# A decoder layer's long convolution: columns ordered feature first, gathering copies on ScalarE, ternary weights in 48 pieces

## What is computed

```
x = x + attention(layernorm(x))                       # 16 query heads, 4 value heads
x = x + conv(ctx, ctx, layernorm(x))                  # 32 heads of 8 rows, 64 x 512 in all
x = x + ffn(layernorm(x))                             # 512 -> 2048 -> 512

# conv, one head, l runs over 512 positions (the context is transposed into them):
kv[i, j, l] = k[i, l] * v[j, l]                       # here k = v, so (i, j) and (j, i) agree
y[i, j]     = causal_conv(kv[i, j], ssm_kernel[h]) + D[h] * kv[i, j]
out[j, l]   = sum_i y[i, j, l] * q[i, l]

# ffn: weights w -> clip(round(w / mean|w|), -1, 1) * mean|w|; activations to 8 bits
```

## Time and profile before

| what | value |
|---|---|
| median of 3 runs (lowest, highest) | 736.14 us (735.43, 736.41) |
| the profiled execution | 736.74 us, span of its instructions 734.9 us |
| busy over the span | PE 86%, DVE 76%, ACT 60%, POOL 36% |
| mean granted TensorE clock | 0.96 |

### The profile page before, as it was taken

How to read it: one execution, slowest core, us unless ns; L and a number is a source line. 1 busy time by engine, 2 the same in 40 slices (tenths; PEclk the granted TensorE clock), 3 DMA queues, 4 the chain that set the end, 5 groups by cost and what they waited for, 6 DMA issues and landing times.

```text
span 734.9 us, 10711 instructions
## 1 busy us (share of the span) xinstructions
PE 635.0 (86%) x3055; PEld 354.8 (48%) x3074; DVE 556.8 (76%) x981; ACT 440.3 (60%) x751; POOL 265.3 (36%) x248
## 2 busy tenths in 40 slices
PE   5899999999999988877778787974789999999995
PEld 3435454554545434655556565652344444444442
DVE  3465756767583644488787888999999999999983
ACT  2446675676667551666666666421676767767781
POOL 1001010000100030555554555642565655656672
PEclk9969999999999969999999999995999999999998
DMA  9535072543618150444535544220001011010001
GB/s 315 143 136 116 1 229 50 178 100 128 171 57 229 44 143 0 153 159 132 181 118 148 170 130 124 85 86 15 15 16 58 29 43 43 29 57 29 15 30 43
DMA packets 34245, 72.51 MB, mean 99 GB/s; under 512 B 4336, under 2 KB 16112, under 8 KB 32560
## 3 DMA queue, kind: packets, MB, share of 16 engines
q1 hardware_dynamic: 31056, 60.72, 28.0%
q10 hardware_dynamic: 3168, 11.54, 4.9%
HBM read 47.51 MB, written 4.28 MB: 70 GB/s over the span
## 4 chain that ended last, share of the span: by engine, by line
DVE 26%; issue 11%; ACT 9%; POOL 6%; PE 5%; ACTq 1%; DVEq 1%; POOLq 0%
POOL big L790 6%; DVE qo L758 4%; ACT wst L848 4%; DVE toep L1184 3%; DVE xq L1170 3%; DVE mb L1188 3%; PE ps L1061 2%; PE ps L1049 2%; DVE act8t L1220 2%; ACT wt L852 2%; ACT ys L829 2%; DVE x_all L1133 1%; DVE mx L1155 1%; DVE xn L1151 1%; DVE st L1138 1%
## 5 line engine op out<-in xcount | busy, mean ns | idle before, releaser
L705 PE MATMUL ps<-kv,toep 128*128 128x288 f32 x640 | 165.4, 416 | 35.5 <-DVE big L750 33.5
L705 PEld LDWEIGHTS ps<-kv,toep 128*128 128x128 f32 x640 | 121.4, 193 | 79.6 <-issue 47.7
L1061 PE MATMUL ps<-wt,xqt 128*128 128x512 bf16 x496 | 122.1, 389 | 11.1 <-DVE toep L1184 9.5
L758 DVE TENSOR_REDUCE qo<-big 128x2048 f32 (+1 forms) x32 | 124.2, 3881 | 0.0
L1313 POOL TENSOR_TENSOR big<-toep,wst 128x512 f32<-128x512 f32 x64 | 81.6, 1276 | 59.5 <-DVE toep L1184 59.4
L393 ACT ACTIVATE big<-ps,kscale 128x512 f32<-128x512 f32 x128 | 85.2, 696 | 13.6 <-PE ps L243 11.9
L243 PE MATMUL ps<-qx,kx 128*128 128x512 f32 x128 | 78.2, 639 | 11.2 <-ACT big L393 10.4
L790 POOL TENSOR_TENSOR big<-ys,qd 128x768 f32<-128x768 f32 x32 | 55.4, 1732 | 85.9 <-ACT ys L830 68.6
L1061 PEld LDWEIGHTS ps<-wt,xqt 128*128 128x128 bf16 x512 | 48.6, 100 | 67.0 <-DVE toep L1184 11.2
L747 DVE TENSOR_TENSOR big<-ps,qd 128x1024 f32<-128x1024 f32 x32 | 39.1, 1223 | 38.2 <-ACT ys L830 37.3
L1049 PE MATMUL ps<-wt,act8t 128*128 128x512 bf16 x253 | 60.8, 386 | 7.8 <-DVE act8t L1220 7.7
(11 more groups left out here) (121 smaller groups left out, 1011.8 us busy)
## 6 DMA issues: line engine op xcount, KB each, us to landing
qx<-kv SPq DMA_DIRECT2D x128, 128.0 KB, 2.4
wst<-in_wall SPq DMA_DIRECT2D x12, 1024.0 KB, 6.0
wst<-in_wall ACTq DMA_DIRECT2D x22, 512.0 KB, 4.6
toep<-krows SPq DMA_DIRECT2D x32, 256.0 KB, 3.4
ctx<-in_ctxt SPq DMA_DIRECT2D x32, 192.0 KB, 2.4
out_y<-ot SPq DMA_DIRECT2D x16, 256.0 KB, 2.0
conv_part<-qo SPq DMA_DIRECT2D x14, 256.0 KB, 2.7
x_all<-in_x SPq DMA_DIRECT2D x2, 1536.0 KB, 14.4
```

The source lines that it names most:

```text
L705: mm = pe.matmul(m.ps[:, LB * r + lb, :].rearrange("p (b s) -> p b s", s=WIDE)[:, :, 0:PAIRS], m.toep[r][:, d * P:(d + 1) * P], m.kv[r][:, ...
L758: nc.vector.tensor_reduce(qo[:, :, bass.ds(h * HD, HD)], z[r].rearrange("p n s j -> p n j s"), AX.X, ALU.add).then_inc(s_red.sem, 1)
L1061: mm = pe.matmul(bank[:, n % 2, :], xqt[r][:, k, :], wt[:, k, n * C:(n + 1) * C], start=(k == 0), stop=(k == CK - 1))
```

## The change

1. The 36 products of a head are ordered feature first and distance second: eight features with four distances each, then the four products of distance 4. The kernel and the transposed context, the Toeplitz product and its 288 columns stay. The writes of L693 and L834 step over four elements.
2. `z[r]` is ordered (feature j, distance s), so that `add_up` adds adjacent elements. L747 writes runs of four; L750 and L790 write with eight elements between neighbours.
3. ScalarE's copies `empty` read PSUM with four elements between neighbours and write `ys[r]` as before.
4. The ternary weights are made in 48 pieces of 512 columns, three in each turn of two heads, in all 16 turns, the last three behind `empty(31)`. In a head the order is `empty`, `squares`, a piece, `double`; the first head of a turn has a second piece behind `double`. `wst` has four slots, of which three are used for pieces.
5. All piece loads are issued by SyncE, between the Toeplitz and context loads. The gain load waits for all 48 pieces, TensorE's first feed-forward product for 32, the first down product for 48.
6. In HBM `wall` is laid out as 48 pieces of 128 x 512, and the loads of the attention stage gather four of them.

The diff, cut to its core:

```diff
@@ SyncE, attention
-            sp.dma_start(wst[:, r, :], wall[r]).then_inc(d_ws[r].sem, 16)
+            sp.dma_start(wst[:, r, :].rearrange("p (b n) -> p b n", n=C),
+                         wall[r * 4:(r + 1) * 4].rearrange("b p n -> p b n")).then_inc(d_ws[r].sem, 16)
@@ context_products
-    whole = nc.gpsimd.tensor_tensor(kv[:, :, first * HD:HD * HD // 2].rearrange("p n (d i) -> p n d i", i=HD),
+    whole = nc.gpsimd.tensor_tensor(window(kv, first, (PAIRS, LB * B), (1, n), (HD // 2, HD)),
@@ convolve
-    z = [... .rearrange("p (n i j) -> p n i j", i=HD, j=HD) for r in range(2)]
+    z = [... .rearrange("p (n j s) -> p n j s", j=HD, s=HD) for r in range(2)]
@@ multiply
-        nc.vector.tensor_tensor(z[r][:, :, 0:H, :],
-                                y[:, :, 0:H * HD].rearrange("p n (d j) -> p n d j", j=HD),
-                                window(q, 0, (2 * HD, NB), (1, H), (1, HD)), ALU.mult)
-        nc.vector.tensor_tensor(z[r][:, :, H, :].rearrange("p n (a j) -> p n a j", j=H),
+        nc.vector.tensor_tensor(z[r][:, :, :, 0:H],
+                                y[:, :, 0:H * HD].rearrange("p n (j d) -> p n j d", d=H),
+                                window(q, 0, (2 * HD, NB), (1, HD), (1, H)), ALU.mult)
+        nc.vector.tensor_tensor(z[r][:, :, :, H].rearrange("p n (a j) -> p n a j", j=H),
@@ add_up
-        nc.vector.tensor_reduce(qo[...], z[r].rearrange("p n s j -> p n j s"), AX.X, ALU.add)
+        nc.vector.tensor_reduce(qo[...], z[r][:], AX.X, ALU.add)
@@ sync of convolve
+        def weights(i, s, first=False):
+            if not first:
+                sp.wait_ge(s_tern.sem, 3 * i + s - 2)
+            sp.dma_start(wst[:, s, :], wall[bass.ds(3 * i + s, 1)] ...).then_inc(d_wc[s].sem, 16)
         with sp.Fori(1, PR - 1) as i:
-            for r in range(2):
-                toeplitz(i, r)
-                context(i + 1, r)
+            toeplitz(i, 0)
+            context(i + 1, 0)
+            toeplitz(i, 1)
+            weights(i, 0)
+            weights(i, 1)
+            context(i + 1, 1)
+            weights(i, 2)
@@ multiply_shifted
-            nc.gpsimd.tensor_tensor(z[r][:, :, HD - SHIFTS:HD, :],
+            nc.gpsimd.tensor_tensor(z[r][:, :, :, HD - SHIFTS:HD].rearrange("p n j s -> p n s j"),
@@ empty
-            y = sums(r)[:, :, HD:H * HD].rearrange("p n (d i) -> p n d i", i=HD)
+            y = sums(r)[:, :, 0:H * HD].rearrange("p n (i d) -> p n d i", d=H)[:, :, 1:H, :]
@@ squares
-            act.activation(m.kv[r].rearrange("p l (b s) -> p (l b) s", s=PAIRS)[:, :, 0:HD],
+            act.activation(window(m.kv[r].rearrange("p l n -> p (l n)"), 0, (PAIRS, NB), (H, HD)),
                            m.ctx[r][:, :, 0:HD], ACT.Square).then_inc(s_sq.sem, 1)
@@ scalar of convolve
+        def turn(i, first=False):
+            for r in range(2):
+                empty(2 * i + r, r, first)
+                squares(2 * i + r + 2, r, i + 2)
+                ternary(i, 2 * r)
+                double(2 * i + r + 2, r)
+                if r == 0:
+                    ternary(i, 1)
...
         for r in range(2):
             empty(H2 - 2 + r, r)
+        for s in range(3):
+            ternary(PR - 1, s)
@@ tensor of ffn
-        pe.wait_ge(m.s_tern.sem, 2 * WCH)
+        pe.wait_ge(m.s_tern.sem, PIECES * 2 // 3)
```

More of the change, by code:

```diff
@@ L50 @@
 WCH = 12
+PIECES = WCH * FF // C
 LN_EPS, RMS_EPS, SUB_EPS, Q_EPS = 1e-5, 1.1920929e-07, 1e-6, 1e-5
@@ L183, in _ @@
                 wait(sp, s_abs, i - 2, r + 1)
-                sp.dma_start(wst[:, r, :], wall[bass.ds((i - 1) * 2 + r, 1)].rearrange("o p n -> (o p) n")
+                sp.dma_start(wst[:, r, :].rearrange("p (b n) -> p b n", n=C),
+                             wall[bass.ds((i - 1) * 8 + r * 4, 4)].rearrange("b p n -> p b n")
                              ).then_inc(d_ws[r].sem, 16)
@@ L724, in convolve @@
     NB = LB * B
-    HALF = FF // 2
     wst = m.wst
+    wt = m.wt.rearrange("p a (b n) -> p (a b) n", n=C)
     qo = m.qo.rearrange("p l b n -> p (l b) n")
@@ L729, in convolve @@
     qd = [sb(f"qd{r}", [P, NB, 2, HD]) for r in range(2)]
-    z = [m.big[:, (2 + r) * FF:(3 + r) * FF].rearrange("p (n i j) -> p n i j", i=HD, j=HD) for r in range(2)]
-    d_wc = [sig("d_wc0"), sig("d_wc1")]
+    z = [m.big[:, (2 + r) * FF:(3 + r) * FF].rearrange("p (n j s) -> p n j s", j=HD, s=HD) for r in range(2)]
+    d_wc = [sig(f"d_wc{s}") for s in range(3)]
     s_ys, s_qd, s_z1, s_z2, s_red = (sig(n) for n in ("s_ys", "s_qd", "s_z1", "s_z2", "s_red"))
@@ L773, in context @@
             load_context(sp, m, ctxt, 2 * i + r, r)
-        for r in range(2):
-            load_weights(sp, 0, r)
-        with sp.Fori(1, PR - 1) as i:
-            for r in range(2):
-                toeplitz(i, r)
-                context(i + 1, r)
+        def weights(i, s, first=False):
+            if not first:
+                sp.wait_ge(s_tern.sem, 3 * i + s - 2)
+            sp.dma_start(wst[:, s, :], wall[bass.ds(3 * i + s, 1)].rearrange("o p n -> (o p) n")
+                         ).then_inc(d_wc[s].sem, 16)
+        for s in range(3):
+            weights(0, s, first=True)
+        with sp.Fori(1, PR - 1) as i:
+            toeplitz(i, 0)
[5 more added lines that the diff above has]
+            weights(i, 2)
         for r in range(2):
             toeplitz(PR - 1, r)
+        for s in range(3):
+            weights(PR - 1, s)
     def gpsimd(pool):
@@ L842, in double, with ternary @@
                      ).then_inc(s_qd.sem, 1)
-        def ternary(n, r):
-            act.wait_ge(d_wc[r].sem, (n + 1) * 16)
+        def ternary(i, s):
+            n = 3 * i + s
+            act.wait_ge(d_wc[s].sem, (i + 1) * 16)
             apart(act)
-            act.activation(wst[:, r, :], wst[:, r, :], ACT.Identity, bias=m.magic[:, 0:1],
+            act.activation(wst[:, s, :], wst[:, s, :], ACT.Identity, bias=m.magic[:, 0:1],
                            scale=m.wscale[:, bass.ds(n, 1)]).then_inc(s_rnd.sem, 1)
-            act.wait_ge(s_rnd.sem, 2 * n + r + 1)
+            act.wait_ge(s_rnd.sem, n + 1)
@@ L851, in ternary @@
             apart(act)
[L852 to L857, removed]
+            act.activation(wt[:, bass.ds(n, 1), :].rearrange("p o n -> p (o n)"),
+                           wst[:, s, :], ACT.Sign, bias=m.magic[:, 1:2]).then_inc(s_tern.sem, 1)
@@ L859, in scalar @@
+        def turn(i, first=False):
[6 more added lines that the diff above has]
+                    ternary(i, 1)
         for r in range(2):
             double(r, r, first=True)
[L861 to L878, removed]
+        turn(0, first=True)
@@ L879, in scalar @@
+        with act.Fori(1, PR - 1) as i:
+            turn(i)
         for r in range(2):
             empty(H2 - 2 + r, r)
+        for s in range(3):
+            ternary(PR - 1, s)
     def vector(dve):
@@ L1043, in down @@
         def down(t, first=False):
-            if not first:
+            if first:
+                pe.wait_ge(m.s_tern.sem, PIECES)
+            else:
                 wait(pe, s_fin, t - 1, 1)
```

14 lines of the change are left out of this document (6 added, 8 removed).

## The result

The changed kernel takes 686.64 us (median of 4 runs, 686.38 to 686.77), the kernel before, measured beside it, 736.26. The ratio is 0.9328 (95% interval 0.9312 to 0.9344), 49.6 us less. The profiled execution took 686.38 us.

The account below looks back on a forecast made before the run. A loop of waits between ScalarE and GpSimd was taken to set the pace. At 5.25 us a head and a 19.2 us hand-over, the first product comes 36.6 us earlier: 699.5 us from 736.14, range 689 to 714.

Parts of the forecast that it names:

- the price of the gathering copies: ScalarE's L829 and L830 reading PSUM with four elements between neighbours: 0.67 us more a head, giving 5.25 us a head.
- the free gather: Rival: ScalarE's strided PSUM reads cost nothing extra; 4.95 us a head, end at 691.1 us; chance 33%.
- Strided writes: GpSimd's L693 and L790, ScalarE's L834, VectorE's L750 writing with gaps: taken as no extra cost.
- The other end, 77%: Upper end for strided writes: 0.49 us each on L790 and L693, 0.16 to 0.20 on L834 and L750.
- The reduction: VectorE's L758 over 2048 elements, adjacent instead of every eighth: 2.26 us instead of 3.886.
- a price per result: Possible reduction cost for each result; argued away because 8 more results came with 256 elements at no visible cost.
- The loop: Waits between ScalarE and GpSimd in the convolution stage: 9.18 us a pair of heads without gather cost.
- TensorE's floor: Convolution matmuls: one every 0.244 us, so a head needs 4.89 us, a pair 9.78 to 10.
- The hand-over: End of convolution 30 to the feed-forward's first product L1184: 19.2 us instead of 24.5.
- The feed-forward: Stage behind the convolutions: keeps its code, with no change of time counted after its first product.
- SyncE's queue: Loads in fixed order: Toeplitz loads have 1.2 us of cover; late-load rival up to 5.5 us a head, 707 us, 5%.
- attention's loads: Attention stage's weight loads: the same 1 MB in shorter rows, a whole turn to land, costed at nothing.

Follow-up runs that it names:

- layout_only: Kernel before with only the new column order and gathering copies; weights stay 24 halves of 1024 columns, loaded from ScalarE's queue: 726.48 us, ratio 0.9869.
- weights_only: Changed kernel with the column order taken back, so only the weights in 48 pieces and their loads on SyncE's queue remain: 711.96 us, ratio 0.9678.
- warm_short: Changed kernel with 5 matmuls that nobody reads in TensorE's idle time before the feed-forward's first rows: 687.51 us, ratio 0.9336.
- warm: Changed kernel with 12 matmuls that nobody reads in TensorE's idle time before the feed-forward's first rows: 693.93 us, ratio 0.9427.
- the parts alone: The column order without the 48 weight pieces (726.48 us), and the 48 pieces without the column order (711.96 us).

## Why the prediction was wrong, point by point

**The step that failed is the price of the gathering copies.** The prediction took 0.67 us a head for it and so 5.25 us as the pace, which is 8.4 of the 12.9 us between forecast and result (699.5 against its own 691.1 without the price). The runs showed 0.00: 0.905 and 0.397 us in the kernel, and 586 ns at every step from PSUM. The row it was taken from, the strided reduction, reads SBUF, and the difference is the memory: ScalarE itself pays 0.47 us for the same step in SBUF. The prediction's own rival, the free gather at 33%, is what happened.

A rule seemed to bear it out. The Trainium skill (SBUF — State Buffer, on "cachelines") gives PSUM lines of 8 bytes and says that patterns that are not contiguous slow down matmuls there; its two accesses to a line are said of SBUF. The prediction carried both over to ScalarE's reads of PSUM, and for those the runs show no cost up to a step of 32 bytes. For SBUF the passage calls a step of four fp32 free; here that step costs ScalarE 1088 ns for 617. There the measurement differs, and decides.

**Strided writes: the wrong end was taken.** They were priced at nothing, on the ground that a write need not hold up its engine; they do, and cost 0.27 us in the squares, 0.22 in L753, 0.15 in L696 and 0.03 in L800 (1.759 for 1.733). The other end, 77%, was exceeded where ScalarE and VectorE write (0.16 and 0.20 us had been its prices), and was far too high for GpSimd (0.49). That the mistake did no harm is luck: TensorE, which none of these engines held up between 296 and 443 us, hides it. No run took the strided writes away.

**The reduction: right.** 2.256 us against 2.26. The argument against a price per result was weaker than it reads: in its two rows elements and results grow together (512 and 16, 768 and 24), so they can't be told apart. The 2.256 us for 256 results settle it.

**The loop: right.** An added copy of 0.47 us gave 5.10 us a head where the walk gives 5.06 ((9.18 + 2 x 0.47) / 2; 5.12 with the 0.53 assumed); all pieces in the loop gave 6.21 where it gave 6.2; a strided reduction gave 5.51 from head 2 to head 30 where it gave 5.54. A piece takes 0.79 and 0.72 us for 0.82 and 0.73.

**TensorE's floor: mis-sized by 0.09 us a head.** With the gather free the prediction had 4.95 us a head, between its floor and the wait for GpSimd's products. Measured were 4.86 (135.97 / 28), TensorE's pace alone; ScalarE's 0.5 to 0.6 us of waiting a pair was slack, not pace. That is 2.6 us over 28 heads. With a start of convolution 2 at 301.95 instead of 302.45, and 5.0 us instead of 5.09 for convolution 30, the first product came at 461.88, not 465.3.

**The hand-over: right.** The first product came 19.0 us behind the end of convolution 30 (about 442.9), forecast 19.2, and TensorE's clock decided its last steps. The gain load was issued at 453.49 us and landed at 458.12, in 4.6 us instead of 7.6, and no one waited for it.

**The feed-forward: left at no change, it took 1.8 us less.** That and the 3.4 us above are the 5.2 us between the two traces that the rival's 691.1 leaves; in medians it is 4.5 us, because the profiled execution of before lay 0.6 us above its median and that of after 0.3 below. The range ended 2 us below 691, so it missed. The traces show where the 1.8 us lie. The first of the 16 outputs (L1228, after L1233) starts 40.12 us behind the first product before, 39.36 after. There the second product follows the first by 4.31 us instead of 5.55, and 1.09 of the difference is one step of VectorE, told in the last section. The shorter reduction brings it: layout_only has 4.32, weights_only 5.58. The larger part is between the 14th and the 15th output, 9.34 us before and 7.94 after, the place told under warm_short. There the 16 matmuls took 5.01 us before, at a granted 0.72 (721.2 to 726.4 us):

```profile
721.27 5.01 PE L1049 MATMUL ps<-wt,act8t 128*128 128x512 bf16 x16 [1.39 <-DVE act8t L1220]
```

In the profiled executions the fall of the clock there comes in the kernel before, layout_only, warm and warm_short (9.34 to 9.63 us), and not in weights_only and both traces of the changed kernel (7.94). It goes with neither part of the change, since warm and warm_short are the changed kernel with matmuls added some 200 us earlier. So 1.4 us of the gain can't be credited to the change. Why the clock fell in some and not in others stays open.

**SyncE's queue, attention's loads: right.** As forecast, no wait of TensorE for a load in the middle stretch. The loads of the attention stage in shorter rows take 6.8 us for 6.0, hidden.

## What to carry to other kernels

When two bounds lie close together, price a change at both of them: here the parts alone gained 9.6 and 24.1 us and together 49.6. Before a stride is priced, ask which memory it steps through; a gather that is needed belongs in the read of PSUM, where it was free, and not in SBUF. Work that must go somewhere goes into the wait of its own engine's queue: one copy further on, the same pieces cost 38 us. A difference of 1 to 2 us is compared stage by stage before it is put down to an edit: here the granted clock in one stretch of 6 us, far behind the edit, was worth as much.

## What had not been expected of the hardware

ScalarE and VectorE read PSUM at steps of 1, 2, 4 and 8 elements in the same time (586 and 690 to 691 ns for 512), while in SBUF four elements between neighbours cost 0.35 to 0.47 us more for 512, and eight hardly more than four. GpSimd differs from the two: its reads cost 24% more at a step of 8 bytes already and 45% at 16, its writes nothing at 8 and 6% at 16.

VectorE's normalising step beside GpSimd's first product took 1.63 us before and 0.54 after, the same instruction. In the order of time of before and of after:

```profile
511.09 1.63 DVE L1151 TENSOR_SCALAR xn<-x_all,mv,rs 128x512 f32<-128x512 f32 x1
```

```profile
462.48 0.54 DVE L1156 TENSOR_SCALAR xn<-x_all,mv,rs 128x512 f32<-128x512 f32 x1
```

Before, GpSimd's product began 0.09 us behind it (511.18) and took 1.26 us; VectorE's step ended 0.28 us behind the end of the product (512.72 and 512.44). After, the product began 0.23 us behind it (462.71) and took 1.46 us, and the step was not held up. The same 0.28 us is found where the step begins during the product: at 470.67 us of after it takes 1.15 us beside a product that runs from 470.24 to 471.53. So it looks as if VectorE's step waits for the end of the product once that is under way, and as if 0.09 us of lead were too little and 0.23 enough; no run was made for it.
